# Two FFNs with tokens sorted by expert in memory instead of every expert for every token

## The reference

```python
x = x + 0.5 * _L0_ffn_ref(_layernorm(x), gate_w, w_gate, w_up, w_down, sw_gate, sw_up, sw_down)
x = x + _L0_attn_ref(_layernorm(x), Wq, bq, Wk, bk, Wv, bv, Wo, bo, head_mask)
x = x + 0.5 * _L0_ffn_ref(_layernorm(x), gate_w, w_gate, w_up, w_down, sw_gate, sw_up, sw_down)

def _L0_ffn_ref(x, ...):
    scores = softmax(x @ gate_w.T)                      # [8192, 8]
    topk_w, topk_i = top_k(scores, 2)
    topk_w = topk_w / (topk_w.sum(-1, keepdims=True) + 1e-20) * 2.5
    combine = zeros((8192, 8)).at[arange(8192)[:, None], topk_i].set(topk_w)
    g = silu(einsum('td,edf->etf', x, w_gate)) * einsum('td,edf->etf', x, w_up)     # 8 experts, f = 176
    y = einsum('te,etd->td', combine, einsum('etf,efd->etd', g, w_down))
    return y + silu(x @ sw_gate) * (x @ sw_up) @ sw_down                            # shared, f = 352
```

## Time and profile before

| what | us |
|---|---|
| runs | 1900.55, 1905.25, 1913.27 |
| median | 1905.25 |
| span of the profiled execution | 1899.1 |
| median less span | 6.2 |

### The profile page before, as it was taken

How to read it: one execution, slowest core, us unless ns; L and a number is a source line. 1 busy time by engine, 2 the same in 40 slices (tenths; PEclk the granted TensorE clock), 3 DMA queues, 4 the chain that set the end, 5 groups by cost and what they waited for, 6 DMA issues and landing times. The chain is left out here.

```text
span 1899.1 us, 30193 instructions
## 1 busy us (share of the span) xinstructions
PE 1755.1 (92%) x9569; PEld 1100.5 (58%) x9600; DVE 1391.1 (73%) x2393; ACT 1237.0 (65%) x1914; POOL 891.2 (47%) x878
## 2 busy tenths in 40 slices
PE   5999999999968888888888888888889999999999
PEld 4887878787843333333333333333368787878776
DVE  5666766676758888888888888888457666766674
ACT  4666566656537777777777777776756566656654
POOL 5666666666732222232333322231146566656665
PEclk9999999999969999999999999999899999999999
DMA  3000100010020111111111111110001010000000
GB/s 101 23 22 25 34 22 23 21 33 22 29 81 2 53 53 54 53 54 53 53 54 53 53 42 54 53 48 24 7 28 34 23 34 12 33 22 33 11 22 12
DMA packets 42270, 69.60 MB, mean 37 GB/s; under 512 B 8508, under 2 KB 10036, under 8 KB 42164
## 3 DMA queue, kind: packets, MB, share of 16 engines
q1 hardware_dynamic: 37360, 66.20, 10.5%
q0 software_dynamic: 4096, 1.08, 0.3%
q10 hardware_dynamic: 708, 0.98, 0.1%
HBM read 28.36 MB, written 12.58 MB: 22 GB/s over the span
## 5 line engine op out<-in xcount | busy, mean ns | idle before, releaser
L934 POOL TENSOR_TENSOR ffn_hid_low<-ffn_hidden,ffn_hid_high 128x512 fp32r<-128x512 f32 x448 | 580.1, 1295 | 367.8 <-ACT ffn_hid_high L860 366.5
L1489 DVE TENSOR_REDUCE attn_neg_max<-attn_p_score 128x2 f32<-128x1024 f32 x512 | 623.4, 1223 | 120.1 <-PE attn_p_score L1201 118.0
L1341 ACT ACTIVATE attn_exps<-attn_p_score 128x1024 f32<-128x1024 f32 x512 | 520.4, 1025 | 217.2 <-PE attn_p_score L1187 215.4
L851 ACT ACTIVATE ffn_silu<-ffn_p_gate 128x512 f32<-128x512 f32 x448 | 266.1, 594 | 269.4 <-PE ffn_p_gate L748 267.5
L994 DVE TENSOR_TENSOR ffn_gated<-ffn_silu,ffn_p_up 128x512 f32<-128x512 f32 x352 | 241.3, 686 | 176.3 <-PE ffn_p_up L748 121.2
L860 ACT ACTIVATE ffn_hid_high<-ffn_hidden 128x512 fp32r<-128x512 f32 x448 | 280.8, 627 | 123.4 <-DVE ffn_hidden L1001 121.3
L1201 PE MATMUL attn_p_score<-k_pack,q_pack 32*128 32x512 f32 x1024 | 259.6, 506 | 53.1 <-ACT attn_exps L1341 37.4
L1218 PE MATMUL attn_p_o<-attn_exps,values 128*32 128x512 f32 x2048 | 278.0, 614 | 6.8 <-ACT attn_o_raw L1347 2.5
L1187 PE MATMUL attn_p_score<-q_pack,k_pack 32*128 32x512 f32 x1024 | 254.0, 503 | 1.5 <-DVE attn_neg_max L1489 1.5
L1001 DVE TENSOR_TENSOR ffn_hidden<-ffn_gated,ffn_p_spread 128x512 f32<-128x512 f32 x352 | 241.4, 686 | 17.8 <-remote 5.6
L1187 PEld LDWEIGHTS attn_p_score<-q_pack,k_pack 32*128 32x128 f32 x1024 | 95.1, 184 | 265.6 <-issue 236.9
(11 more groups left out here) (213 smaller groups left out, 2069.0 us busy)
## 6 DMA issues: line engine op xcount, KB each, us to landing
q_pack<-attn_q_high SPq DMA_DIRECT2D x32, 256.0 KB
k_pack<-attn_k_high SPq DMA_DIRECT2D x32, 256.0 KB
feed_x_in<-in_x SPq DMA_DIRECT2D x16, 256.0 KB, 2.8
ffn_x_res<-in_x SPq DMA_DIRECT2D x16, 256.0 KB, 3.4
after_ffn<-ffn_x_out SPq DMA_DIRECT2D x16, 256.0 KB, 2.0
attn_x_in<-after_ffn SPq DMA_DIRECT2D x16, 256.0 KB, 2.8
k_pack<-attn_k_low SPq DMA_DIRECT2D x16, 256.0 KB
q_pack<-attn_q_low SPq DMA_DIRECT2D x16, 256.0 KB
```

The source lines that it names most:

```text
L851: nc.scalar.activation(silu[f % 2][0:n, :], p_gate[f % 2][0:n, :], ACT.Silu).then_inc(silu_ready, 1)
L934: nc.gpsimd.tensor_tensor(hid_low[s][0:n, :], hidden[s][0:n, :], hid_high[s][0:n, :].bitcast(F32), ALU.subtract).then_inc(low_ready, 1)
L1341: nc.scalar.activation(exps[n % len(exps)][:], score_bank("exp", b, n)[:], ACT.Exp, scale=inv_sqrt)\
L1489: V.tensor_reduce(neg_max[g % 2][:, j:j + 2, t], score_bank("max", b, n)[:], AX.X, ALU.max, negate=True).then_inc(max_read, 1)
```

## The change

Both FFNs become three blocks each, and a queue in memory lies between them.

Setup also packs each expert's weights, high and low, into 1280 columns and stores them to memory (`own_weights`, 8 x 128 x 1280, 5.24 MB).

`dispatch` loads all of x into one buffer `mid` (64 tiles of 128 tokens), makes the statistics of all of it, one power on POOL (`send_rstd`, 128x64), and then goes through 8 pairs of batches. For each it normalises and turns the tokens, makes the logits, the shared expert's 3 tiles (gate, up, down as before, its low parts now on DVE), and adds half of its output to `mid`. On DVE it finds each token's two experts and their weights, and PE counts, by matmuls with two constant matrices in bf16, how many tokens stand ahead of each in its expert's list (`rank`), which gives a place in that expert's region of `rows`. POOL then writes each token's normalised row with its number, rank and weights (132 values, 528 bytes) to its two places by indirect DMAs of 128 rows each, 16 a pair. At the end DVE makes tables of the blocks' places and experts, and SP fills the rest of each region's last block with rows from a constant (8 DMAs whose place is read from a table).

`experts` runs 39 blocks of 512 rows. SP reads place and expert of a block from the tables, loads its rows (264 KB) and its expert's weights (640 KB), each into one of three buffers; PE turns the rows, makes gate and up of the first 128 hidden units and one product that holds gate and up of the other 48 (`p_rest`), and the down product: 14 matmuls of 128x512. DVE scales each row of the output with its token's weight, and POOL scatters the rows, 4 indirect DMAs of 128 rows of 512 bytes a block, to the token's two places in `results`.

`collect` loads both results of each token, POOL adds them, DVE adds half of the sum to `mid`, SP stores. In FFN1 it also clears attention's buffers on DVE and makes attention's first batch. The attention loses its `feed_pieces`.

The core of the diff. `ffn` and `Feed` go:

```diff
-                n, s = width(f), slot(b, f)
-                pool.wait_ge(high_ready, b.count(TILES, f + 1))
-                nc.gpsimd.tensor_tensor(hid_low[s][0:n, :], hidden[s][0:n, :],
-                                        hid_high[s][0:n, :].bitcast(F32), ALU.subtract).then_inc(low_ready, 1)
...
-                V.tensor_tensor(hidden[slot(b, f)][:], gated[f % 2][:], p_spread[:], ALU.mult).then_inc(weighted_ready, 1)
```

`dispatch` comes, here its PE order, POOL's program, the end of DVE's pass and SP's:

```diff
+            for j in range(-2, NPAIR + 1):
+                for s in range(2 * STILES):
+                    n = 2 * STILES * j + s
+                    if shared_pair(j):
+                        gate_up(j, n)
+                    if 0 <= n - LAG < TILES_ALL:
+                        down(n - LAG)
+                    if s == 0 and shared_pair(j + 1):
+                        logits(j + 1)
...
+                    if s == 4 and shared_pair(j + 1):
+                        rank(j + 1)
...
+            pool.wait_ge(var_ready, 1)
+            nc.gpsimd.tensor_tensor(moment["rstd"][:], moment["var_eps"][:], w.minus_half[:], ALU.pow).then_inc(rstd_ready, 1)
+            for j in range(NPAIR):
+                pool.wait_ge(rows_ready, j + 1)
+                pool.wait_ge(moved, j + 1)
+                for t in range(NT2):
+                    for choice in range(2):
+                        nc.gpsimd.indirect_dma_start(
+                            queue.rows, bass.IndirectOffsetOnAxis(ap=g.slots[j % XRING][:, choice, t:t + 1], axis=0),
+                            rows[j % XRING][:, t, :], None).then_inc(scattered[j % XRING], 16)
...
+            for e in range(E):
+                at = sp.value_load(queue.pads_from[0:1, e:e + 1], min_val=0, max_val=E * CAP - BLK)
+                sp.dma_start(queue.rows[bass.ds(at, BLK), :], queue.pad[e * BLK:(e + 1) * BLK, :]).then_inc(padded, 16)
+            sp.wait_ge(padded, 16 * (E + 1))
+            for i in range(XRING):
+                sp.wait_ge(scattered[i], SCATTERS * 16 * len(range(i, NPAIR, XRING)))
```

`experts` comes, here the order of PE, POOL and DVE and the loads:

```diff
+                row = sp.value_load(queue.row_of[0:1, i:i + 1], min_val=0, max_val=E * CAP + (SPARE - 1) * BLK)
...
+                sp.dma_start(rows[i % 3][:], queue.rows[bass.ds(row, BLK), :].rearrange("(p t) c -> p t c", t=NT))\
+                    .then_inc(rows_loaded[i % 3], 16)
...
+                    project(p_gate, i, 0).then_inc(gate_ready, 1)
+                    need(pe, gated, i)
+                    project(p_up, i, P).then_inc(up_ready, 1)
+                if 0 <= i - 2:
+                    turn_y(i - 2)
+                if i < NBLK:
+                    need(pe, gated_rest, i)
+                    project(p_rest, i, 2 * P).then_inc(rest_ready, 1)
+                if i + 1 < NBLK:
+                    turn_x(i + 1)
+                if 0 <= i - 1 < NBLK:
+                    down(i - 1)
...
+                for t in range(NT):
+                    nc.gpsimd.indirect_dma_start(
+                        queue.results, bass.IndirectOffsetOnAxis(ap=to_row[i % 4][:, t:t + 1], axis=0),
+                        y[i % 3][:, t, :], None).then_inc(sent[i % 3], 16)
...
+                    V.tensor_tensor(hidden[:], silu[i % 2][:], p_up[:], ALU.mult).then_inc(gated, 1)
...
+                    V.tensor_tensor(low[i % 2][:], hidden[:], high[i % 2][:].bitcast(F32), ALU.subtract).then_inc(low_ready, 1)
...
+                    V.tensor_tensor(hidden_rest[0:REST, :], silu_rest[64:64 + REST, :], p_rest[64:64 + REST, :], ALU.mult)\
+                        .then_inc(gated_rest, 1)
+                if i + 1 < NBLK:
+                    x_low(i + 1)
```

More of the change, by code:

```diff
@@ L130, in setup @@
[L130 to L134, removed]
-        block = ctx.enter_context(nc.Block())
[L136 to L145, removed]
+        own_gate, own_up = sb("own_gate", [P, E, F]), sb("own_up", [P, E, F])
@@ L147, in _ @@
+        splits += [(attn_loaded, 16 * 9, wq[:], w.wq[0][:], w.wq[1][:]),
+                   (attn_loaded, 16 * 9, wk[:], w.wk[0][:], w.wk[1][:])]
+        OWN = 10
         @block.sync
         def _(sp):
[L149 to L156, removed]
@@ L163, in _ @@
[L163 to L175, removed]
+            sp.dma_start(own_gate[:], dram["w_gate"].rearrange("p (e f) -> p e f", f=F)).then_inc(own_loaded, 16)
@@ L183, in _ @@
[L183 to L190, removed]
+            act.dma_start(gate[:], dram["sw_gate"]).then_inc(shared_loaded, 16)
@@ L693, in ffn @@
-        silu_ready, gated_ready, weighted_ready = sem("silu_ready"), sem("gated_ready"), sem("weighted_ready")
+        sem = lambda n: nc.alloc_semaphore(name=f"{name}_{n}")
+        ring = lambda make, n, count, *a: [make(f"{n}{i}", *a) for i in range(count)]
+        stats = sb("stats", [P, TOKENS, 6])
+        moment = {n: sb(n, [P, TOKENS]) for n in
+                  ("mean_sum", "mean_diff", "m2", "mean", "diff2", "var_within", "var_eps", "rstd", "shift")}
+        rows = ring(sb, "rows", XRING, [P, NT2, RW])
@@ new lines, in turn_x, with logits @@
+            def turn_x(k):
+                pe.wait_ge(normed, k + 1)
+                need(pe, xt_copied, k)
+                for t in range(NT):
+                    at = k % 2 * NT + t
+                    last = nc.tensor.transpose(p_turn[:, t * P:(t + 1) * P], rows[k // 2 % XRING][:, at, 0:D], w.ident[:])
+                last.then_inc(x_turned, 1)
+            def logits(j):
+                pe.wait_ge(xt_copied, 2 * j + 2)
+                need(pe, rows_ready, j)
+                for t in range(NT2):
+                    half, cols = t // NT, slice(t % NT * P, (t % NT + 1) * P)
+                    last = nc.tensor.matmul(p_route[:, t * E:(t + 1) * E], xt[j % 2][:, half, cols], w.gate_w[:],
+                                            start=True, stop=True)
+                last.then_inc(logits_ready, 1)
@@ new lines, in norm_apply @@
+            def norm_apply(k):
+                j = k // 2
+                act.wait_ge(shift_ready, 1)
+                need(act, scattered[j % XRING], SCATTERS * 16 * (j // XRING))
+                need(act, x_turned, 2 * (j - XRING) + 2)
+                for t in range(NT):
+                    at = k * NT + t
+                    last = nc.scalar.activation(rows[j % XRING][:, k % 2 * NT + t, 0:D], mid[:, at, :], ACT.Identity,
+                                                bias=moment["shift"][:, at:at + 1], scale=moment["rstd"][:, at:at + 1])
+                last.then_inc(normed, 1)
```

1394 lines of the change are left out of this document (723 added, 671 removed).

## The result

The changed kernel takes 1917.2 us in the median of 18 runs (1912.3 to 1922.0) beside 1905.1 for the kernel before on the same chips: a ratio of 1.0062, 95% interval [1.0045, 1.0079]. It is 0.6% slower, within the one per cent that was named as no change. The forecast was 1924 and 1.0% slower.

A forecast was written before the change was run, and what follows sets the result against it. Matmul count on PE was taken to bound the FFNs. By stage, 36 + 2 x (232 + 234) + 62 + 46 + 833 + 9 = 1918, and 6.2 from span to median gave 1924 us; range 1825 to 2135.

The forecast's parts named there:

- 9 us of borders: Between stages: six borders at about 1.5 us each beside the stores, 9 us in the sum.
- c: POOL's time per scatter in dispatch and experts, the deciding unknown: between 0.58 and 3.1 us, taken as 1.34.
- the forecast's case: Dispatch and experts: POOL's scatters set the pace, c between 1.25 and 1.5, time 1873 to 2015 us; chance 0.46.
- rival B: Dispatch and experts: rows set POOL's scatter price, c from 1.5 on; 2128 us at c = 1.7; chance 0.12.
- Rival D: Dispatch and experts: POOL holds each scatter until it has landed, c = 1.7, 2128 us; chance 0.03.
- The Trainium skill's fit: POOL's DMAs: about 2.0 us plus bytes/436e3; as POOL's pace c = 2.15, near 2386 us; not used in the sum.
- The lead-in's 47: Start of dispatch: loads, statistics, power, first pair's normalising and logits, and routing, all exposed, together 47 us.
- POOL again sets the pace by a little: Experts: POOL's four scatters, 5.36 us a block, exceed the DVE and PE chain of 5.1; 5.46 with the semaphore.
- Rival A: Dispatch and experts: POOL is hidden, c up to 1.2, DVE or the chain sets the pace; 1852 us; chance 0.32.
- the 6 us I took off: Attention: FFN2's feed leaves its last batch, so 6 us (0 to 10) come off, giving 833.
- Rival C: Experts: TensorE's clock held at the half level, a block 8.2 us, 2135 us in all; chance 0.07.
- the expected 242 us per FFN: Both FFNs: 1038 fewer matmuls at 0.233 us each, 242 us of PE gone per FFN.

The follow-up runs named there:

- the run with both: Changed kernel with dispatch's hidden product in PSUM, pad stores shared by SP and ACT, and attention's clearings between collect's additions: 1899.6 us, ratio 0.9962 to the kernel before.

## Why the prediction was right, and where it was not

The time and the side came out, and the sum by stage holds within 9 us in each stage, where the forecast has 9 us of borders beside the stages and the measured stages include them. But the size does not deserve the trust that 1924 beside 1917 suggests.

**c.** I took 1.34 as the geometric middle of 0.58 and 3.1. From first to last scatter dispatch needs 170.2 for 127 distances, 1.340 each, and POOL waits for nothing: the forecast's case there. The agreement is luck in part. The upper end stood on a price by rows, and the runs showed that rows cost about 0.001 us each: rival B's mechanism is wrong, and the number is 1.27 us a scatter, of which some 1.13 comes with the instruction, plus the holds by DVE. Rival D falls too: a scatter leaves every 1.27 us though it lands 2.3 us (rows) or 3.3 us (results) after issue. The Trainium skill's fit (page "DMA: Bandwidth & Descriptors", section "Anatomy of one DMA — SWDGE (gpsimd) path"), taken there as POOL's pace, would have been off by 470 us; it is worded per DMA, and its 2.15 is near the 2.3 to landing of rows, though not the 3.3 of results.

**Dispatch.** POOL is the pace, as forecast. The next engine is DVE at 18.4 a pair, my 19. The lead-in's 47 was right to a microsecond, and it was the largest thing that could be taken away. That the block ends on the pad stores was right too: SP waits 2.7 and 2.5 us for them at the ends of the two dispatches, after all else. But the size, 12 for them and 2 for landing, was too much, since they start 5 us ahead of the last scatter: from the start of the last scatter to the next block it is 8.3 and 6.9 us, border included.

**Experts.** The step that failed: "POOL again sets the pace by a little". Rival A's mechanism holds here. POOL needs 4 x 1.27 = 5.08 and lies under a chain of 5.35 which I had put at 5.1; the forecast's 5.46 came close for the wrong reason. Of the 0.25 that was missing, 0.10 lies in the first product: with its hand-off I counted 1.62 for gate and up, where gate, 0.97 to the silu's start, and the silu, 0.75 to the hidden product, stand on the chain, and the up product beside them. Another 0.10 I took off for the first pass without a row for it, and the last 0.05 or so is rounding, since my terms add up to 5.26 and not 5.2. The other hand-offs were as counted: 0.24 for five, beyond their passes, at 0.05 each.

**Collect 1** was mis-sized, 70.7 for 62. With the clearings moved, 4 came back of the 9 I gave them; the chain of attention's front is long on its own, and I had priced only its last steps.

**Attention and the clock.** 831.8 for 833. In the profiles of the changed kernel and its ten variants, none of which touches attention, the stage took between 831 and 839, so the 6 us I took off are no more than its spread. Rival C did not come: the granted clock is 1.00 in the middle of the experts with PE at 82%. It fell elsewhere, to 0.91 over the scatters of dispatch and 0.50 in collect, where PE is not the pace.

**The chances** were less good than the time: half stood on slower by over 1%, 0.15 on what came.

**Where the expected 242 us per FFN went:** 17 us beyond them came back in the first, as 48 of lead-in, 170 of POOL's scatters, 8 to the dispatch's end, 240 of experts, in whose middle PE is busy 82%, and 71 of collect: 537. Before, normalising, routing and loading lay under the matmuls, with PE busy 99.9%.

## What to carry to other kernels

Work that is halved on the busiest engine uncovers what lay beneath it: price the new stage by its longest chain and by the count of instructions on each engine, not by the work removed. An indirect DMA has a price per instruction on its issuing engine, so count the instructions and put as many rows as possible into each. Two things that end close together hide each other: an edit that takes away either alone left the dispatch within its spread, and only the run with both shortened it clearly.

## What the runs showed of the hardware

A scatter on POOL can be held by a DVE pass with two SBUF operands that runs when the scatter starts. Of the 42 long scatters, 34 end 0.84 or 0.85 us after such a pass does: 24 beside the low part of the hidden product, 10 beside that of the turned tokens. With one operand of the first in PSUM, those 24 are gone, and the 12 long ones left all stand beside the second. The number of SBUF operands is not the whole of it: four of the 42 end 0.86 to 0.89 after the hidden product's own pass, which reads one. The Trainium skill, page "SBUF — State Buffer", section "SBUF: two separate sides", has a port pair that a DVE instruction with two SBUF inputs and a POOL instruction that reads SBUF lock against each other. The trace agrees for the 34; the four are outside what it says.

The hold can also make POOL keep step. In the experts POOL's four scatters need 5.08 us by themselves, yet they showed 5.34 a block without a wait, exactly DVE's, because in the block shown, and in most others, two scatters meet a low part on DVE: the idle time of 0.42 ahead of 322.27 lasts until the low part's end at 322.30, and the scatter of 1.09 ends at 325.90, 0.84 after L1016. With 64 rows the two holds grew, to 0.58 of idle time and a scatter of 1.17, and the block was 5.35 again. An engine that shows no wait need not set the pace; leaving its work out did settle it.
